# The tail of a windowed-attention and mixture-of-experts block, passed through in chunks of 10 image rows

## The reference, cut to what matters

```python
def _L0_conv_ref(x, w_qkv, b_qkv, w_proj, b_proj):      # 8 heads of 16 channels, window K = 17, PAD = 8
    qkv = xt @ w_qkv.T + b_qkv
    q, k, v = jnp.split(qkv, 3, axis=2)
    k_w, v_w = windows(k), windows(v)                   # 17 x 17 patches, zero outside the image;
                                                        # flat.reshape(B, K2, C, L) mixes channel and position
    attn = softmax(einsum('bhnc,bhnlc->bhnl', q, k_w), axis=-1) * mask_w[:, None]
    out = einsum('bhnl,bhnlc->bhnc', attn, v_w)
    return out @ w_proj.T + b_proj

def _moe(tokens, router_w, w1, b1, w2, b2):             # 8 experts, top 2
    probs = softmax(tokens @ router_w.T)
    rw, re = top_k(probs, 2); rw = rw / max(rw.sum(-1), 1e-12)
    combine = zeros((N, 8)).at[arange(N)[:, None], re].set(rw)
    out = tokens
    for e in range(8):
        out = out + combine[:, e:e+1] * (gelu(tokens @ w1[e] + b1[e]) @ w2[e] + b2[e])
    return out

x = x + _L0_conv_ref(_ln_c(x), ...)
t = _to_tokens(x)
t = t + _L0_ffn_ref(_ln_t(t), ...)
```

## Time and profile before

| | us |
|---|---|
| median of 3 runs | 480.82 |
| all runs | 480.62, 480.82, 484.02 |
| the profiled execution's own time | 485.29 |
| its span | 483.5 |
| busy: TensorE matmul 438.1, weight load 306.9, VectorE 319.2, ScalarE 264.9, GpSimd 194.3 | |
| matmuls | 6970 records, two for one fp32 matmul |

### The profile page before, as it was taken

One profiled execution on the slowest core, in us unless ns is written; L12 is line 12 of the kernel. 1 busy time (PEld: TensorE's weight loads), 2 busy tenths in 40 slices (PEclk: granted clock), 3 DMA queues, 4 the chain that ended last, 5 costly groups with the idle time before them and its releaser, 6 DMA issues.

```text
span 483.5 us, 16599 instructions
## 1 busy us (share of the span) xinstructions
PE 438.1 (91%) x6970; PEld 306.9 (63%) x6970; DVE 319.2 (66%) x797; ACT 264.9 (55%) x465; POOL 194.3 (40%) x249
## 2 busy tenths in 40 slices
PE   4899937389899999999999999995899999999996
PEld 2789934157677777767766677774555545855553
DVE  1240173459999899989988889983387646264553
ACT  2240083948889998999999986862000000361332
POOL 9403044166866655556666786744000000001110
PEclk9785556779999999999999999999799757679999
DMA  6069995836666575767565654478640000007400
GB/s 195 21 217 292 212 298 175 275 89 212 198 207 204 205 235 170 225 220 218 193 216 187 207 173 161 176 206 225 225 68 0 2 0 0 1 0 272 157 17 35
DMA packets 39480, 77.24 MB, mean 160 GB/s; under 512 B 9412, under 2 KB 26453, under 8 KB 38589
## 3 DMA queue, kind: packets, MB, share of 16 engines
q1 hardware_dynamic: 38542, 74.61, 48.9%
q0 software_dynamic: 144, 1.36, 0.8%
q10 hardware_dynamic: 720, 0.22, 0.2%
HBM read 45.76 MB, written 29.29 MB: 155 GB/s over the span
## 4 chain that ended last, share of the span: by engine, by line
PE 82%; issue 8%; POOL 4%; DVE 3%; DMA 1%; ACT 1%; POOLq 0%; SPq 0%; DVEq 0%; ACTq 0%
PE ps L805 19%; PE ps L880 10%; PE ps L828 9%; PE ps L850 7%; PE ps L810 6%; PE ps L919 4%; PE ps L770 4%; PE ps L939 3%; PE ps L831 3%; PE ps L763 3%; PE ps L836 2%; PE ps L726 2%; PE ps L874 2%; PE ps L731 2%; PE ps L892 1%
## 5 line engine op out<-in xcount | busy, mean ns | idle before, releaser
L805 PE MATMUL ps<-slabs 128*32 128x401 f32 x528 | 119.5, 519 | 21.6 <-POOL slabs L529 20.4
L805 PE MATMUL ps<-prb,slabs 128*32 128x401 f32 x494 | 116.0, 522 | 0.0
L1064 DVE CUSTOM_DVE_ANT_0 scn<-ps,con 128x401 f32<-128x401 f32 x120 | 65.1, 571 | 35.1 <-PE ps L810 35.1
L670 ACT ACTIVATE exb<-scn,lowest 128x401 f32<-128x401 f32 x120 | 74.2, 621 | 11.3 <-DVE lowest L1064 11.2
L810 PEld LDWEIGHTS ps<-con,slabs 128*32 128x32 f32 x960 | 43.5, 113 | 50.0 <-issue 48.7
L1054 DVE COPY_PREDICATED slabs<-con,zt 128x1152 f32<-128x1152 int32 x41 | 67.2, 1640 | 0.1
L810 PE MATMUL ps<-con,slabs 128*32 128x128 f32 x960 | 62.7, 280 | 1.2 <-issue 1.1
L522 POOL TENSOR_TENSOR slabs<-con,qrot 128x192 f32<-128x192 f32 (+4 forms) x67 | 31.2, 468 | 80.8 <-DVE slabs L1054 76.1
L579 POOL TENSOR_TENSOR xln<-xln,wide 128x400 f32<-128x400 f32 x4 | 4.9, 1230 | 138.7 <-DVE wide L1228 138.7
L659 ACT ACTIVATE prb<-slabs 64x1169 f32<-64x1169 f32 x40 | 47.2, 1180 | 14.3 <-DVE slabs L1054 13.7
L587 ACT ACTIVATE prb<-wide 128x400 f32<-128x400 f32 x8 | 4.3, 537 | 87.6 <-DVE wide L988 87.3
(11 more groups left out here) (139 smaller groups left out, 757.5 us busy)
## 6 DMA issues: line engine op xcount, KB each, us to landing
slabs<-zsl SPq DMA_DIRECT2D x40, 539.5 KB, 4.0
zsl<-uv SPq DMA_DIRECT2D x44, 484.5 KB, 3.6
slabs<-combd SPq DMA_DIRECT2D x2, 1600.0 KB, 8.2
ebs<-zsl SPq DMA_DIRECT2D x4, 539.5 KB, 7.5
slabs<-kimd SPq DMA_DIRECT2D x2, 881.7 KB, 12.6
vimd<-vimg SPq DMA_DIRECT2D x1, 1612.0 KB, 5.7
xt<-x_in SPq DMA_DIRECT2D x8, 200.0 KB, 7.0
frd<-wide SPq DMA_DIRECT2D x2, 800.0 KB, 6.0
```

The source lines that it names most:

```text
L670: nc.scalar.activation(v(ex[x & 1], a, (1, NC3)), v(scn, (x & 1) * NB * NC3 + a, (1, NC3)), ACT.Exp, scale=-1.0, bias=lowest[:, NB * (x & ...
L805: mm(bank(g, (1, NC3), parts=TW, p0=TW * i), w, v((kt, kh)[b & 1][x & 1], b // 2 * C, (1, NC3)), start=first, stop=False, skip_group_check ...
L1064: nc.vector.tensor_tensor_reduce(v(scn, i * NC3, (1, NC3)), bank(g, (1, NC3)), cv("pos"), 1.0, 3e38, ALU.add, ALU.min, lowest[:, i:i + 1]) ...
```

## The change

In the front, nothing but constants: `head_of` and the rows of `wp_t` take another order, `slot_of` (56 columns) takes the place of `sel`, `iota` runs from -8. Four small VectorE instructions ahead of the main loop make `mmat` (identity minus 1/128) and `wpm` (the projection with its column means taken off). At the loop's end, `eb_rows(0)` goes ahead of the last `products`, the reciprocal of `den` goes to iteration 40, and the first `product` to iteration 42.

The tail then goes chunk by chunk in an order written out by hand for each engine:

- `turn_out` writes chunk 0 of `frot` first (2 x 200 KB), then the rest (2 x 600 KB); `turn_in(k)` reads back per chunk, 9 DMAs in all; chunk 0 waits only for its own writes. TensorE adds the turned image into the sum bank with `perm` (`turned_back`), so `sbd` is not added by VectorE.
- V's boundary terms: per chunk four groups `j`, members cc = j, j+4, j+8, j+12. One vector instruction makes the products of all members (up to 4 x 400 columns on 120 partitions). VectorE makes `VD` = 3, 3, 2, 2 groups of chunks 0 to 3 into two buffers, GpSimd the other six (`late_product`) from a copy of the edge sums in SBUF, into two buffers of its own. `vsum` adds each member on 32 columns of the array of its own.
- Centring by products: bank `CENB[k]` gets `mmat` times (x + bias) plus `wpm` times attention; ScalarE squares it and copies it out. The same attention also starts y's bank (`y_start`), so y needs no residual of its own; GpSimd prepares x + bias + normed tokens (`start_sum`), and one VectorE addition ends the chunk.
- The router runs in three parts (chunk 0, chunk 1, chunks 2 and 3), 17 links each: the top two by comparison of logits, the second weight by ScalarE's Tanh of their difference.
- Weights of chunks 0 and 1 come by `spread`; those of chunks 2 and 3 through memory, after the last router part. The hardware loop is gone.

```diff
+            def turn_out(a, z, done):
+                for i in range(2):
+                    sp.dma_start(dv(frd, i * C * L + a * Q, (L, C), (1, (z - a) * Q)), frot[:, a * Q:z * Q]).then_inc(done, 16)
...
+            turn_out(0, 1, S["rot_first"])
+            turn_out(1, NQ, S["rot_out"])
+            sp.wait_ge(S["inj_ready"], SZ)
+            sp.wait_ge(S["rot_first"], 32)
+            turn_in(0)
             sp.wait_ge(S["rot_out"], 32)
+            for k in range(1, NQ):
+                turn_in(k)
...
+            result(0)
             sp.wait_ge(S["comb_copied"], NQ)
+            sp.dma_start(dv(combd, 2 * Q, (L, E8), (1, 2 * Q)), v(pm[1], 0, (1, 2 * Q), parts=E8)
+                         ).then_inc(S["comb_out"], 16)
             sp.wait_ge(S["comb_out"], 16)
+            sp.wait_ge(S["vused_late"], vlate(NQ - 1, VGROUPS - 1) + 1)
+            for k in range(2, NQ):
+                sp.dma_start(v(slabs, (k - 2) * E8 * Q, (Q, E8), (1, Q)),
+                             dv(combd, k * Q, (0, C), (L, E8), (1, Q))).then_inc(weights_in[k - 2], 16)
...
+            def turned_back(k):
...
+                pe.wait_ge(nat_in[k], 16 * len(TURNED[k]))
+                mm(bank(NATB[k], (1, Q)), cv("perm"), v(sbd, k * Q, (1, Q)), start=True, stop=False, skip_group_check=True)
+            def vsum(k, j):
...
+                for m in range(members(j)):
+                    n8 = live(j + VGROUPS * m)
+                    src = v(slabs, late_buf(n) + m * Q, (1, Q), parts=n8) if late else v(pr[n & 1], m * Q, (1, Q), parts=n8)
+                    last = mm(bank(NATB[k], (1, Q), parts=TW, p0=TW * m), cv("slot_of", (1, TW), off=24 - 8 * j, parts=n8), src,
+                              start=False, stop=(j + VGROUPS * (m + 1) >= HC - 1 and j >= 2), skip_group_check=True)
...
+            eb_rows(1); eb_rows(2); rn_rows(0); rn_rows(1); turned_back(0); vsum(0, 0); vsum(0, 1)
+            turned_back(1); vsum(0, 2); vsum(0, 3); x_part(0); rn_rows(2); vsum(1, 0); att_part(0)
+            vsum(1, 1); rn_rows(3); variance(0); vsum(1, 2); rstd_rows(0); logits(0); vsum(1, 3)
+            up(0, 0); up(0, 1); turned_back(2); vsum(2, 0); x_part(1); y_start(0); spread(0, 0)
+            comb_rows(0); y_bias(0); spread(0, 1); step(0, 0); att_part(1); vsum(2, 1); step(0, 1)
+            variance(1); vsum(2, 2); step(0, 2); logits(1); rstd_rows(1); vsum(2, 3); step(0, 3)
+            eb_rows(3); turned_back(3); step(0, 4); vsum(3, 0); vsum(3, 1); step(0, 5)
+            vsum(3, 2); vsum(3, 3); step(0, 6); x_part(2); att_part(2); step(0, 7); x_part(3); att_part(3)
+            up(1, 0..2); comb_rows(1); spread(1, 0); variance(2); variance(3); y_start(1); y_bias(1)
+            spread(1, 1); step(1, 0); logits(2); logits(3); rstd_rows(2); rstd_rows(3)
+            step(1, 1..7), with comb_rows(2); comb_rows(3) after step(1, 5)
+            for k in range(2, NQ): y_start(k); y_bias(k); step(k, 0..7)
...
+            # VectorE, after product(0, 0) in the loop
+            product(0, 1); product(0, 2); product(1, 0); attend(0); product(1, 1); rstd(0)
+            product(1, 2); norm(0); route_first(0); attend(1); route_rest(0); product(2, 0)
+            weighted(0, 0); product(2, 1); weighted(0, 1); rstd(1); weighted(0, 2); norm(1)
+            weighted(0, 3); attend(2); route_first(1); weighted(0, 4); product(3, 0); route_rest(1)
+            weighted(0, 5); product(3, 1); weighted(0, 6); attend(3); weighted(0, 7); finish(0)
+            rstd(2); weighted(1, 0); norm(2); weighted(1, 1); norm(3); weighted(1, 2)
+            route_first(2); weighted(1, 3); route_rest(2); weighted(1, 4..7); finish(1)
```

More of the change, by code:

```diff
@@ L236, in program @@
         qhalf = kimg
-        rexp = zt
+        rexp = exb
         bqr, bqn, bk2, bp = sb("bqr", SZ), sb("bqn", 1), sb("bk2", 2), sb("bp", 1)
@@ L974, in _ @@
-            with pe.Fori(1, NQ - 1) as k:
-                chunk(k, False)
-            chunk(NQ - 1, True)
+            eb_rows(1)
+            eb_rows(2)
+            rn_rows(0)
+            rn_rows(1)
+            turned_back(0)
+            vsum(0, 0)
+            vsum(0, 1)
+            turned_back(1)
+            vsum(0, 2)
+            vsum(0, 3)
+            x_part(0)
+            rn_rows(2)
+            vsum(1, 0)
+            att_part(0)
+            vsum(1, 1)
+            rn_rows(3)
@@ new lines, in _, with step @@
+            variance(0)
+            vsum(1, 2)
+            rstd_rows(0)
+            logits(0)
+            vsum(1, 3)
+            pe.wait_ge(S["w_late"], 16 * 7)
+            up(0, 0)
+            up(0, 1)
+            turned_back(2)
+            vsum(2, 0)
+            x_part(1)
+            y_start(0)
+            spread(0, 0)
+            comb_rows(0)
+            y_bias(0)
+            spread(0, 1)
+            def step(k, e):
+                t = E8 * k + e + (3 if k else 2)
+                if t < E8 * NQ and (k or t < E8):
+                    up(t // E8, t % E8)
+                down(k, e)
+                if k < 2 and e + 2 < E8:
+                    spread(k, e + 2)
@@ new lines, in _ @@
+            step(0, 0)
+            att_part(1)
+            vsum(2, 1)
+            step(0, 1)
+            variance(1)
+            vsum(2, 2)
+            step(0, 2)
+            logits(1)
+            rstd_rows(1)
+            vsum(2, 3)
+            step(0, 3)
+            eb_rows(3)
+            turned_back(3)
+            step(0, 4)
+            vsum(3, 0)
+            vsum(3, 1)
+            step(0, 5)
+            vsum(3, 2)
+            vsum(3, 3)
+            step(0, 6)
+            x_part(2)
@@ new lines, in _ @@
+            att_part(2)
+            step(0, 7)
+            x_part(3)
+            att_part(3)
+            for e in range(3):
+                up(1, e)
+            comb_rows(1)
+            spread(1, 0)
+            variance(2)
+            variance(3)
+            y_start(1)
+            y_bias(1)
+            spread(1, 1)
+            step(1, 0)
+            logits(2)
+            logits(3)
+            rstd_rows(2)
+            rstd_rows(3)
+            for e in range(1, E8):
+                step(1, e)
+                if e == 5:
+                    comb_rows(2)
+                    comb_rows(3)
```

663 lines of the change are left out of this document (427 added, 236 removed).

## The result

The changed kernel takes 521.4 us (median of 4 runs, 515.99 to 525.64); the kernel before took 481.32 beside it. The ratio of those runs is 1.0784, 95% interval 1.0672 to 1.0895: slower by 8%, where the forecast was 462.4 and 453 to 473. The profiled execution has a span of 521.8 us against the forecast 465.1, so 56.7 us have to be found (521.8 - 465.1).

What follows compares the result with a forecast made beforehand. TensorE's serial chain behind the main loop was taken as the bound. Following the new order to 462.3 plus 2.8 of hand-overs gave span 465.1; the 18.4 saved, taken from median 480.82, gave 462.4 us, range 453 to 473.

Steps and rivals of the forecast that it cites:

- the price of V's groups: V's boundary sums: 16 groups of up to four 32-column matmuls at 0.68 us, 10.9 us instead of 40.2.
- Tiles of unequal height don't overlap: Rival, chance 0.05: V's boundary stays at 40.2 instead of 10.9, +29, about half absorbed by idle time: 478.
- Half clock in part: Rival, chance 0.15: waits and thin tiles drop the clock for some 10 us of TensorE-bound work, +5 to 10: 470.
- step 8: Hand-overs behind waits, weight loads and semaphores not hidden: some 14 places at 0.2 each, 2.8 us, span 465.1.
- Steps 1 and 2: Loop's end and turned image: frot written out from 343.4, first chunk's image back at 351.3, TensorE idle some 4.5 us.
- the later image (352 to 354): Turned image's first reads queue behind the other 1.2 MB of writes, making the result 1 to 3 us later.
- Step 3: First chunk, from the turned image to its router's end: 351.3 to 372.0, 20.7 us.
- Step 4: Chunk 0's expert steps, with a TensorE wait for product(3,1) behind nine router links: 372.0 to 404.7, 32.7 us.
- Step 5: Chunk 1, from centring through router links and expert steps to the comb copies: 404.7 to 429.4.
- step 6: Weights of chunks 2 and 3 through memory: 2.2 write, 6.3 first load, in at 437.9; new TensorE stall 4.9.
- The weights don't bind: Rival, chance 0.1: comb rows are early or the weight load lands sooner, saving 4.9: 457.5.
- Step 7: The end, from weights in at 437.9 to the last finish at 459.3, then finish and output to 462.3.

Runs made afterwards that it cites:

- single-file run: Changed kernel with 120 rows for every member of a V group, all members on the same 32 columns of the array: 507.61 us (one run).
- even heights: Changed kernel with 120 rows for every member of V's groups, zeros in the selection blocks for rows that don't belong: 478.18 us, ratio 0.9886 to before.
- kernel before at full height: Kernel before, with products and sums of all 15 V boundary rounds on 120 partitions, no tiles, no new order: 467.96 us, ratio 0.968.
- mended chunk order: Changed kernel with 120-row members, product(3,1) ahead of router links, chunk 2's weights by spreads, chunk 0's turned image added after its third group: 464.05 us.
- old order with even tiles: Kernel before, stage by stage over all chunks, with only the V part exchanged for groups of 32-column, 120-row tiles: 448.35 us, ratio 0.9263.

## Why the prediction was wrong

**The step that failed is the price of V's groups: "four matmuls cost two passes of 0.34, 0.68 us".** The rows it rested on the earlier trace rows show tiles that are all 128 high. Heights of the changed kernel differ within a group, and the price was 2.37 at full clock: 1.69 more, times 16 groups, 27 us, before any clock. The runs showed three passes of 0.79 us in place of two of 0.34. I had this as a rival, "Tiles of unequal height don't overlap", at 0.05, and the one sentence against it, "they share nothing else", was an assertion with no row behind it. It is the line that was wrong: the case for it (nothing in the trace has unequal heights) was the stronger one and asked for a chance near even. The trace showed the best case only, and I took the best case as the price, though I had written the other bound, 40.2, down; between the two the measured 16 x 2.37 = 37.9 lies at the far end. The heights on the last two column groups were also misread: they are 8 to 56 rows, not 24 to 56.

**Its price was wrong too, and joined with another rival.** I gave that rival 478 because idle time would absorb half of 29. The single-file run took 29.4 more than even heights, and nothing was absorbed: TensorE is the chain there. And thin tiles in single file are also thin tiles one at a time, which is the condition of "Half clock in part" (my point against it was "here four tiles run at once"). The two rivals were not alternatives; one brings the other. Together they make 45.4 of the 56.7 us by the spans, 41.0 by the medians: about 25 for the passes and 16 for the clock. The earlier trace rows held the warning (0.50 below 33 rows, TensorE busy throughout), and the run of the kernel before at full height shows that it was the height.

**The rule that I weighed.** The Trainium skill (TensorEngine Tiling (Array Packing), Key Properties) says that changing the tiling mode drains TensorE, and its Tiling Modes section counts 128, 64 and 32 rows as different modes beside the column widths. I counted only changes between full and 32-column tiles. The traces agree with the rule if the height of an operand counts as its mode, which are the changes that I left out: members of 112 and 80 rows in one burst, 48 and 16 each behind a gap of 0.65. It also bears on the rest: two records behind a tile group take 0.87 where two take 0.67 elsewhere, 0.2 for a change that I had priced below 0.1.

**The other steps.** Take the kernel with even heights, whose V groups cost about what was forecast (0.77 to 0.81), and hold it against the steps. The forecast's 2.8 of hand-overs (step 8) is spread over its steps.
- Steps 1 and 2: right within 1 us there (344.2, 351.4); in the changed kernel earlier by 3.0 and 2.4. The idle TensorE ahead of the turned image and the lower clock behind it came as foreseen; the later image (352 to 354) that I had weighed was not seen.
- Step 3: 24.0 for 20.7. Most of it is a wait that I left out. The last five links need the Tanh, and on ScalarE that stands behind the first two Gelus, which wait for vsum(1,3) and an up on TensorE and for a table load. The chain has sum, up, load and Gelus as 1.49, 1.65, 1.28 and 1.08, and from the end of the logits (368.6) to the end of the links 6.8 us pass where I had 4.3. I followed this wait in step 4 and not here.
- Step 4: 42.5 for 32.7, the one other step that is really off. The nine links in front of product(3,1) I took at 0.21 each; with GpSimd at its products beside them two took 1.35 and 2.7 and others 0.7 and 0.9, 6.9 for all nine in place of 2.0, and TensorE waited 8.22. Moving the product ahead gave 6.7 back. Behind that wait the first two records on the chain run at half clock (1.56 and 1.63), which I had not priced either.
- Step 5: 23.0 for 24.7; step 6: 8.2 for 8.5. The new stall by the write and load of the weights was right: 1.64 + 6.58 in the changed kernel, and taking chunk 2 out of it gave 4.4. "The weights don't bind" is refuted.
- Step 7: 24.4 for 21.4. Behind the wait for the weights the first three pairs of records take 1.25 to 1.33 where later ones take 0.67: half clock, 1.9 of the 3.0. I priced half clock behind the first wait and did not behind the one that I had found myself.
- Prices: VectorE's product 1.82 (forecast 1.8), GpSimd's 3.1 for 1600 columns (3.5), table load 1.28, no table of its own for Tanh, a link 0.19 to 0.24 when it is not held. All good.

The span of even heights is thus 11.3 above the forecast, its median 15.8 above 462.4. The other 4.5 are in the last line of my working: I took the difference of spans off the median of before, which lay 4.5 below its profiled execution; the profiled execution with even heights (476.4 and 1.8 around it) lies at its own median, 478.18. Execution against execution, the forecast would have been 466.9.

**What the change is worth.** The V part, tiled at even height, is worth 36 us in the old order (484.44 to 448.35); full height without tiles gave 16 of them. The rest of the change costs more than it gives: even with three of its waits mended it ends at 464.05. Two of its costs were measured and mended: the trip of chunk 2's weights (4.4), which the old order hides behind chunk 0, and the products that meet the router (6.7). The 15.7 us that are left are hardly waits of TensorE. From the end of the loop to the last addition, the mended chunk order (first) and the old order with even tiles:

```profile
340.70:463.20 122.50, 111.65 (x505) 60.52 (x503) 51.31 (x108) 34.79 (x62) 23.76 (x14) 0.87 0.14 41
```

```profile
341.60:444.20 102.60, 94.11 (x440) 53.66 (x440) 59.78 (x93) 29.95 (x52) 19.65 (x10) 0.95 0.26 83
```

TensorE stands still for 10.9 and 8.5 us, nearly the same, but is busy for 17.5 us more. Part of it is the spreads, 24 in place of 8, with 13.3 us of busy time in place of 3.9; part is the clock, 0.87 against 0.95. No run took the order, the router in parts and the norm by products apart, so how the 15.7 divide among them stays open.

## What to carry to other kernels

A matmul on part of the array is priced by the tiles beside it: before counting on two or four at once, look for a row where tiles of just these heights run together, and if there is none, give them all one height, with zeros in the stationary blocks for the rows that don't belong: in these runs more rows cost no time and kept the clock up. Then ask what is left busy. Two of the three mended waits gave 11 us back, and the order was still slower than the old one, with TensorE busy 17.5 us longer. When a rival's condition also brings the condition of another, price the two together and give the pair the chance. And whatever one gives to GpSimd, read what VectorE does beside it: short instructions with two SBUF inputs on the critical chain pay the most.

## What the runs showed of the hardware that was not expected

- Heights of neighbouring 32-column tiles: those of 72 to 120 rows share a pass, 56 and 40 share one, 64 shares none with 96 or 32, and those up to 32 share none with taller ones. A pass is 0.79 at full clock whether it holds one member or two, and a group of four of one class takes 0.77 to 0.81; on the same 32 columns they take 2.80.
- TensorE's granted clock depends on the height of the operands: the same 60 matmuls at 120 rows in place of 120 down to 8 keep 499 ns each, and 16 us of the whole kernel's time go with it (0.968 [0.9616, 0.9744]). At 120 rows on 32 columns, one at a time, the clock was 0.96 from 352 to 372; with 120 and 104, then 56 and 40 rows, 0.59; in the changed kernel 0.64, and 0.50 from 358 to 367, busy without a gap.
- A running GpSimd instruction on SBUF held back VectorE instructions with two SBUF inputs until it ended: 0.19 became 2.68. One with a single SBUF input and 4 elements per partition went from 0.17 to 0.93, while a reduction with a single SBUF input kept its 0.19, and those with a PSUM operand kept their 1.82. The Trainium skill (SBUF — State Buffer, Who interferes with whom) says that a VectorE instruction with two SBUF inputs contends with a GpSimd one that reads SBUF, and that the pair of ports is held for the whole instruction. The trace agrees for the two-input links. The one of 4 elements is a tensor_scalar, for which the page names another condition; whether it was held by that or by what stood before it, no run here tells.
